# Expert attention on one core: projections regrouped on TensorE, value sums side by side, value split moved to VectorE

## What is computed

```python
ss = sigmoid(x @ Ws).reshape(b, t, H, E);  sd = sigmoid(x @ Wd).reshape(b, t, H, E)   # H=8 heads, E=5, DH=64
ms, md = topk_mask(ss, 3), topk_mask(sd, 3)
ss_g, sd_g = ss * ms, sd * md
q5 = (x @ Wq).reshape(b, t, H, E, DH)
k5, v5 = split((x @ Wkv).reshape(b, t, 2, H, E, DH))
q = einsum('bthed,bthe->bhtd', q5, sd_g)
k = einsum('bthed,bthe->bhtd', k5, ss_g)
v = einsum('bthed,bthe->bhtd', v5, ss_g)
attn = softmax(einsum('bhid,bhjd->bhij', q * DH ** -0.5, k))
out = einsum('bhij,bhjd->bihd', attn, v)
o5 = einsum('bthd,dm->bthm', out, Wo).reshape(b, t, H, E, DIM)
y = einsum('bthem,bthe->btm', o5, md)
```

## Time and profile before

| | |
|---|---|
| median of 3 runs | 2641.14 us (2640.59 to 2646.53) |
| the profiled execution, its own time | 2640.06 us |
| its span, first to last instruction | 2638.3 us |
| TensorE busy | 2353.3 us, 89% |
| VectorE busy | 2009.1 us, 76% |
| GpSimd busy | 1804.6 us, 68% |
| ScalarE busy | 1480.1 us, 56% |
| mean granted TensorE clock | 0.953 of full |

### The profile page before, as it was taken

One profiled execution on the slowest core, in us unless ns is written; L12 is line 12 of the kernel. 1 busy time (PEld: TensorE's weight loads), 2 busy tenths in 40 slices (PEclk: granted clock), 3 DMA queues, 4 the chain that ended last, 5 costly groups with the idle time before them and its releaser, 6 DMA issues. The chain is left out here.

```text
span 2638.3 us, 55375 instructions
## 1 busy us (share of the span) xinstructions
PE 2353.3 (89%) x21054; PEld 1517.7 (58%) x21054; DVE 2009.1 (76%) x3656; ACT 1480.1 (56%) x2085; POOL 1804.6 (68%) x1704
## 2 busy tenths in 40 slices
PE   6788777888799999999978999999879799999987
PEld 3555534644466667666655666666533556666655
DVE  7998555545677777777669999999567899999974
ACT  4222122332688888888834566556744256655665
POOL 0888300000699999999946899999820388999986
PEclk9899779889899999999989999999989899999999
DMA  1000000000698989889943666666710256666666
GB/s 46 1 1 0 1 24 14 1 24 17 134 160 151 163 148 162 159 151 163 145 112 64 113 113 117 119 116 113 140 40 0 70 95 117 113 119 116 117 113 122
DMA packets 829353, 243.48 MB, mean 92 GB/s; under 512 B 811528, under 2 KB 820232, under 8 KB 829088
## 3 DMA queue, kind: packets, MB, share of 16 engines
q1 hardware_dynamic: 829088, 239.93, 49.6%
HBM read 20.70 MB, written 1.05 MB: 8 GB/s over the span
## 5 line engine op out<-in xcount | busy, mean ns | idle before, releaser
L2303 PE MATMUL banks<-g_w,normed_t 128*128 128x320 f32 x1536 | 508.7, 457 | 23.9 <-DVE g_scratch L2610 11.0
L1581 POOL TENSOR_TENSOR g_p_lo<-g_p,g_p_hi 128x768 bf16<-128x768 f32 (+1 forms) x256 | 478.5, 1891 | 35.7 <-POOL g_z L2496 23.2
L1786 DVE TENSOR_REDUCE at_negmax<-banks 128x1 f32<-128x1024 f32 x256 | 301.4, 1219 | 154.6 <-PE banks L1698 154.6
L2303 PEld LDWEIGHTS banks<-g_w,normed_t 128*128 128x128 f32 x1536 | 262.3, 189 | 209.9 <-DVE g_scratch L2610 85.8
L1763 POOL TENSOR_TENSOR at_p_lo<-at_p,at_p_hi 128x640 bf16<-128x640 f32 x256 | 356.9, 1415 | 12.9 <-ACT at_p_hi L1751 11.3
L1594 DVE TENSOR_REDUCE g_negmax<-banks 128x1 f32<-128x1024 f32 x256 | 310.3, 1217 | 42.0 <-PE banks L1504 42.0
L1744 ACT ACTIVATE at_p<-banks,at_negmax 128x1024 f32<-128x1024 f32 x256 | 285.7, 1116 | 6.2 <-DVE at_negmax L1786 6.2
L1558 ACT ACTIVATE g_p<-banks,g_negmax 128x1024 f32<-128x1024 f32 x256 | 285.2, 1114 | 5.6 <-DVE g_negmax L1594 5.3
L1698 PE MATMUL banks<-at_k_t,at_q 64*128 64x512 f32 x1024 | 258.0, 622 | 18.2 <-POOL at_k_t L2047 9.5
L1504 PE MATMUL banks<-g_k_t,g_q 64*128 64x512 f32 x1024 | 254.4, 615 | 12.6 <-ACT g_p L1558 7.2
L1571 ACT CAST g_r_hi<-banks 128x256 bf16<-128x256 f32 x128 | 47.7, 372 | 380.8 <-PE banks L1515 380.8
(11 more groups left out here) (419 smaller groups left out, 5995.8 us busy)
## 6 DMA issues: line engine op xcount, KB each, us to landing
at_swapped<-at_crossed SPq DMA_DIRECT2D x128, 128.0 KB, 2.8
g_w<-in_ex_w SPq DMA_DIRECT2D x2, 2880.0 KB, 11.5
f_w<-in_W SPq DMA_DIRECT2D x2, 1024.0 KB, 5.5
at_rope<-in_rope SPq DMA_DIRECT2D x1, 2048.0 KB, 9.4
at_t_hi<-at_p_hi SPq DMA_TRANSPOSE x128, 3.7
at_t_lo<-at_p_lo SPq DMA_TRANSPOSE x128, 3.6
g_t_hi<-g_p_hi SPq DMA_TRANSPOSE x128, 4.3
g_t_lo<-g_p_lo SPq DMA_TRANSPOSE x128, 4.2
```

What stands on the lines that cost most here:

```text
L1581: self.nc.gpsimd.tensor_tensor(self.part(self.p_lo, j, h), self.p[:, j % 2, h, 0:self.WIDTH[h]], self.part(self.p_hi, j, h), ALU.subtract) ...
L1786: self.nc.vector.tensor_reduce(self.negmax[:, j % 2, h:h + 1], self.core.banks[:, first:first + 2, :], AX.XY, ALU.max, negate=True).then_i ...
L2303: nc.tensor.matmul(out[:, 0:ED], core.xt[:, at:at + P], w[:, kind * H + tile // (T * BATCH) * 2 + h, :], start=True, stop=True).then_inc(p ...
```

## The change

It sets another order in the loop's four streams.

- TensorE: the first pair goes ahead of the scores, the second behind them, both in the spare banks. The third goes into banks 0 and 1, once the first exponential of tile j + 1 has emptied them (`exp_done`). The first pair therefore waits only for the product before the last. The scores, which overwrite banks 0 and 1, wait for the third product of the step before. Both value sums follow each other ahead of the third pair. The turning goes into the spare banks, between the value sums, and waits for the second product. `subtract` comes last.
- ScalarE: the first exponential comes before `act_copy`; the placing and the second exponential move up; the cast of the values comes behind the second exponential.
- GpSimd: the values' low part is gone.
- VectorE: it takes that subtraction (`dve_split_values`, between second maximum and routing); first product and sum of values go ahead of the first maximum, the second product between the maxima.

The last unit keeps its order of `subtract`, value sums and copies.

```diff
--- before.py
+++ after.py
@@ -1617,11 +1617,6 @@
         if unit >= 2:
             act.wait_ge(self.av_done, 2 * self.T * (unit - 1))
         self.nc.scalar.copy(self.v_hi[:, unit % 2, self.half(i)], self.v[:, self.half(i)]).then_inc(self.v_split_hi, 1)
-
-    def pool_split_values(self, pool, unit, i):
-        pool.wait_ge(self.v_split_hi, 2 * unit + i + 1)
-        self.nc.gpsimd.tensor_tensor(self.v_lo[:, unit % 2, self.half(i)], self.v[:, self.half(i)], self.v_hi[:, unit % 2, self.half(i)],
-                                     ALU.subtract).then_inc(self.v_split, 1)
 
     def dve_split_values(self, dve, unit, i):
         dve.wait_ge(self.v_split_hi, 2 * unit + i + 1)
@@ -2349,23 +2344,27 @@
             for j in range(STEPS):
                 unit, t = j // T, j % T
                 turning = t in (2, 6) and unit + 1 < UNITS
-
-                def beside(k):
-                    n = first(j) + 2 * k
-                    if n < first(j + 1):
-                        pe.wait_ge(product_ready, n // 2)
-                        for h in range(2):
-                            project(n + h, spare[h])
-
+                pairs = (first(j + 1) - first(j)) // 2
                 finishing = done_in(t) if unit + 1 == UNITS else ()
+
+                def both_heads(k, banks):
+                    for h in range(2):
+                        project(first(j) + 2 * k + h, banks[h])
 
                 if j == STEPS - T:
                     pe.wait_ge(product_ready, first(STEPS) // 2)
+                if t in (3, 7) and unit + 1 < UNITS:
+                    pe.wait_ge(qk_ready, (unit + 1) * 4 + t // 4 * 2 + 2)
+                if pairs:
+                    pe.wait_ge(product_ready, first(j) // 2 - (1 if j and first(j) - first(j - 1) == 6 else 0))
+                    both_heads(0, spare)
                 if j + 1 < STEPS:
-                    if t in (3, 7) and unit + 1 < UNITS:
-                        pe.wait_ge(qk_ready, (unit + 1) * 4 + t // 4 * 2 + 2)
+                    if pairs:
+                        pe.wait_ge(product_ready, first(j) // 2)
                     hs.scores(pe, j + 1)
-                beside(0)
+                if pairs == 3:
+                    pe.wait_ge(product_ready, first(j) // 2 + 1)
+                    both_heads(1, spare)
                 hs.transpose(pe, j)
                 for k, tile in finishing[0:1]:
                     turn_out(k, tile)
@@ -2373,15 +2372,19 @@
                     project_out(*done_in(t - 1)[1])
                 if j:
                     hs.values(pe, j - 1, 0)
-                beside(1)
-                hs.subtract(pe, j)
                 if turning:
-                    pe.wait_ge(hs.exp_done, 2 * j + 3)
+                    pe.wait_ge(product_ready, first(j) // 2 + min(pairs, 2))
                     for i in range(2):
-                        turn(unit + 1, t // 4 * 2 + i, core.ps[i])
+                        turn(unit + 1, t // 4 * 2 + i, spare[i])
+                if unit + 1 == UNITS:
+                    hs.subtract(pe, j)
                 if j:
                     hs.values(pe, j - 1, 1)
-                beside(2)
+                if pairs == 3:
+                    pe.wait_ge(hs.exp_done, 2 * j + 3)
+                    both_heads(2, core.ps[0:2])
+                if unit + 1 < UNITS:
+                    hs.subtract(pe, j)
                 for k, tile in finishing[0:1]:
                     project_out(k, tile)
                 for k, tile in finishing[1:2]:
@@ -2450,23 +2453,26 @@
                 unit, t = j // T, j % T
                 last = j + 1 == STEPS
                 finishing = done_in(t) if unit + 1 == UNITS else ()
-                hs.act_copy(act, j)
+                if unit + 1 == UNITS:
+                    hs.act_copy(act, j)
                 for k, tile in finishing[0:1]:
                     place_out(k)
                 if not last:
                     hs.act_exp(act, j + 1, 0)
+                if unit + 1 < UNITS:
+                    hs.act_copy(act, j)
+                if t in (2, 6) and unit + 1 < UNITS:
+                    for i in range(2):
+                        place(unit + 1, t // 4 * 2 + i, core.ps[6 + i])
                 if not last:
                     hs.act_hi(act, j + 1, 0)
+                if not last:
+                    hs.act_exp(act, j + 1, 1)
                 if t == 0 and unit:
                     hs.act_split_values(act, unit, 1, (v_ready, (unit + 1) * T))
                 if t == 4 and unit + 1 < UNITS:
                     hs.act_split_values(act, unit + 1, 0, (v_ready, (unit + 1) * T + T // 2))
-                if not last:
-                    hs.act_exp(act, j + 1, 1)
                 hs.act_rest(act, j)
-                if t in (2, 6) and unit + 1 < UNITS:
-                    for i in range(2):
-                        place(unit + 1, t // 4 * 2 + i, core.ps[i])
                 if not last:
                     hs.act_hi(act, j + 1, 1)
                 for k, tile in finishing[1:2]:
@@ -2537,10 +2543,6 @@
             for j in range(STEPS):
                 for h in range(2):
                     hs.pool_lo(pool, j, h)
-                if j % T == 0 and j:
-                    hs.pool_split_values(pool, j // T, 1)
-                if j % T == 4 and j // T + 1 < UNITS:
-                    hs.pool_split_values(pool, j // T + 1, 0)
                 if j < 18 and j % 9 < 8:
                     count_duels(2 + j // 9, j % 9)
                 elif j < 18:
@@ -2680,20 +2682,24 @@
                 def beside(k):
                     n = first(j) + 2 * k
                     if n < first(j + 1):
-                        apply_gates(n, 6)
+                        apply_gates(n, 0 if k == 2 else 6)
 
                 finishing = done_in(t) if unit + 1 == UNITS else ()
 
+                beside(0)
+                if j + T < TOTAL:
+                    sum_values(j + T)
                 if j + 1 < STEPS:
                     hs.dve_max(dve, j + 1, 0)
-                beside(0)
+                beside(1)
                 if j + 1 < STEPS:
                     hs.dve_max(dve, j + 1, 1)
                 if unit + 1 == UNITS and t > 2:
                     add_out(*done_in(t - 1)[1])
-                beside(1)
-                if j + T < TOTAL:
-                    sum_values(j + T)
+                if t == 0 and unit:
+                    hs.dve_split_values(dve, unit, 1)
+                if t == 4 and unit + 1 < UNITS:
+                    hs.dve_split_values(dve, unit + 1, 0)
                 if j:
                     route(j - 1)
                 beside(2)
```

## The result

| | before | after |
|---|---|---|
| median | 2643.3 us (4 runs beside after's) | 2700.56 us (2695.86 to 2700.78, 4 runs) |
| ratio, 95% interval | | 1.0212 [1.0194, 1.023] |
| the profiled execution, its span | 2640.06, 2638.3 us | 2695.86, 2694.1 us |
| TensorE, VectorE busy | 2353.3, 2009.1 us | 2353.3, 2024.6 us |
| GpSimd, ScalarE busy | 1804.6, 1480.1 us | 1772.6, 1468.6 us |

A forecast was written before the change was run, and what follows sets the result against it. A closed round over TensorE and VectorE was taken to bound the step, VectorE alone afterwards. Shorter ordinary steps, less turning and splitting costs, made both loops +18 (2658 us); clock falls added 25: 2683 us, range 2646 to 2710.

The forecast's parts named there:

- The ordinary step: Loop step without turning or splitting: VectorE alone sets it, 7.3 us instead of 7.71.
- The turning step: Steps t = 2 and 6: eight transposes between the value sums delay VectorE's reciprocal by 0.9 to 1.0, 8.25 us.
- The splitting step: Steps t = 4 and, from unit 1, t = 0: VectorE's subtraction waits for ScalarE's late cast, 2.5 us more.
- the idle before the subtraction: Sign on VectorE: about 1.8 us idle, released by ScalarE's copy of the values, 26 to 28 times.
- Taking 0.70 and not 1.22: Subtraction's length on VectorE: 0.69 taken, GpSimd then waiting for the routing; 1.22 beside GpSimd would add 14 us.
- The clock: TensorE's 2.7 us holes lower its clock: 18 of 26 counted, 1.4 us each, +25 us.
- The second loop: Second expert attention loop, about 1.5 us longer before the change: +8.3 against the first loop's +9.8.
- In the last 11 steps ... nothing net: Loop's end: the split at j = 56 costs up to 2.5 us, but GpSimd's longest chain is relieved: nothing net.
- the wait that I had said would not come back: Value sums' wait for transposed low parts of the probabilities: these land 2.0 into a step, due at 3.4.
- On GpSimd the removed split gives nothing back: In splitting steps, taking the values' split off GpSimd saves no time.
- my second rival: Stall, clock fall, and VectorE meets GpSimd: subtraction 1.22 (+14) or ordinary step 7.4 (+11); 2694 to 2710, chance 0.16.

The follow-up runs named there:

- The filler: Changed kernel plus two unused fp32 matmuls of 512 columns where TensorE would stand empty, filling 24 of 26 holes: 2677.34 us, ratio 1.0119.

## Why the prediction was right, and where it was short

Forecast 2683 (2646 to 2710), measured 2700.56: slower, as said, 18 us above. Term by term, each against its own step in the prediction:

- **The ordinary step**, forecast 7.3, is 7.21, and 7.28 behind a splitting one. The second and third pairs wait for nothing beyond VectorE's round, and no value sum waited for its operands in the 53 steps. Right.
- **The turning step**, forecast 8.25, is 8.43. The reciprocal waits 0.78 us for the second value sum, as forecast, but this isn't what sets the step. The third product is done at 1674.37, and the scores come at 1674.63, without idle time right behind the first pair: TensorE's own order, with the eight transposes behind a wait of 0.25 us for the second product, is the longer way. The forecast took VectorE's. The run with the turning moved agrees: the reciprocal's wait is gone, and the step is still 8.40.

```profile
1672.39 0.17 DVE L1601 RECIPROCAL g_recip<-banks 128x2 f32<-128x2 f32 x1 [0.78 <-PE banks L1545]
...
1673.55 0.82 DVE L2612 TENSOR_TENSOR g_scratch<-banks,g_gate 128x640 f32<-128x640 f32 x1
...
1673.45 1.24 PE L2298 MATMUL banks<-g_w,normed_t 128*128 128x320 f32 x4
1674.63 1.56 PE L1504 MATMUL banks<-g_k_t,g_q 64*128 64x512 f32 x6
```

- **The splitting step**, forecast 9.8, is 9.86; the idle before the subtraction, forecast about 1.8, is 1.84. One of the 13, at j = 8, has 11.29; the same step was long before the change too (8.98): VectorE's mask comparison stands there, 1.51 us long in both kernels. The run that moves only the cast confirms the cause. Taking 0.70 and not 1.22 was right, for the reason given: GpSimd was waiting for the routing (2.28 us in that step).
- **The clock**, forecast 18 falls of 1.4, +25: 24 of the 26 holes were followed by one. Of the steps behind them 20 grew by 1.36 to 1.60, 1.42 in the mean, the two at j = 17 by only 0.15 and 0.21, since they take 8.70 even at the upper clock: the second mask comparison stands there, 1.50 us long instead of 0.35 before, and two fell into the last nine steps. The filler shows 27.9 in the 53 steps of both loops, 2.9 over the forecast. The size was right. The count was too small, and came near by luck: four of the 24 falls cost next to nothing in these steps or lie behind them.
- **The second loop** was forecast to lose 1.5 less, since it had been that much longer; it lost 24.7 us in the 53 steps and the first one 26.1. Right.
- **"In the last 11 steps ... nothing net"** is the step that failed: +4.1 and +2.9. The late cast stalls VectorE at j = 56 too, and with it the routing and GpSimd, whose chain sets these steps. The waits of 1895 to 1926 show where it surfaces, as the wait that I had said would not come back:

```profile
PE banks L1545 <- DMA g_t_lo<-g_p_lo: 4.2, 2, 3.0
```

  With the cast first the nine steps take 62.4 and 62.4, so the late cast is the cause (ahead of the second exponential it still costs there: 66.0 and 64.4). A part is the clock: the step j = 53, behind the last of the 13 holes, takes 7.97 us, and 6.82 with either earlier cast, where the clock holds. The filler says nothing here, since it leaves that hole open (65.2 and 65.1 us for the nine steps). Behind the 3.0 us wait above the clock fell too; what that cost wasn't taken apart.
- **The lead-in** was not in the sum: +1.35 in each loop, in every kernel with the new order. The first pair now stands ahead of the scores of tile 1; that this is the reason was not tried apart.
- **"On GpSimd the removed split gives nothing back"** was too strong: in the old order it was worth 4.8 and 7.1 us a loop (turning steps 113.2 and 115.3 us, 108.4 and 108.2 with the split moved); 3.4 of the 7.1 are a single step of 12.14, behind whose wait the clock fell.

In sum the loops lost 60.5 where 43 was forecast, 17.5 more: 4.9 in the 53 steps without the clock, 2.9 more clock, 7.0 in the last steps, 2.7 in the lead-ins. The program outside them was 4.7 shorter in the profiled execution. The measured time lies among the numbers of my second rival, but neither of its mechanisms was at work.

## What to carry to other kernels

An instruction moved to the engine that bounds the loop should find its input ready: here 0.7 us of work cost 2.5 because its producer had been put behind an exponential that depends on the same engine, and moving that producer up turned a loss of 57 us into a gain of 27. When an operation is moved, follow its input's place in the producer's order as closely as its own. Price a stall in the last, thinner steps of a loop apart from the steady ones: another engine has the longest chain there, and the cover is gone.

## What the runs showed of the hardware

- A hole's length alone doesn't decide over the clock. Of 26 holes of 2.58 us in the steady steps two were followed by a clock of 1.00. In the kernel with cast first and split on GpSimd one of 2.69 us left it at 1.00 as well (windows: the hole, and what follows):

```profile
1742.30:1745.00 2.70, 0.04 (x1) 0.04 (x2) 1.96 (x3) 1.38 (x2) 2.46 (x3) 1.00 1.14 107
1745.00:1748.40 3.40, 3.40 (x60) 3.07 (x61) 0.83 (x3) 2.03 (x4) 3.09 (x4) 1.00 0.51 109
```

  The holes of 1.57 us in the steady steps were followed by no fall, nor those of 0.86. But in the last nine steps, which have little matmul work, the kernel with the cast first has a hole of 1.55 us in each loop with a fall behind it; the changed kernel has the same hole without one:

```profile
1845.00:1846.50 1.50, 0.00 (x1) 0.00 (x0) 0.51 (x2) 1.50 (x3) 0.86 (x1) 1.00 0.50 99
1846.50:1849.90 3.40, 3.34 (x10) 1.32 (x11) 0.33 (x1) 1.65 (x3) 3.14 (x3) 0.62 1.06 137
```

- The Trainium skill (TensorE: Matmul & The Clock Gate, "HAM oscillation — how this bites in real kernels") describes a kernel whose clock falls again at each DMA wait of its loop, waits of about 3 to 5 us. Here holes of 2.58 us did the same in 24 of 26 cases, at 1.42 us in a step behind them, so a shorter wait can be enough, though not every time.
- Two fp32 matmuls of 512 columns in the hole, with 0.86 us left empty, kept the clock at 2.4 GHz behind all 24 holes that they filled, at no cost to the step.
- The subtraction with both inputs in SBUF took 0.70 us with GpSimd idle, and 1.03 to 1.06 in the steady steps beside it; the longest, in the lead-in, 1.23.
- The mask comparison on VectorE (a tensor_scalar, 128x320 fp32, one tensor input in SBUF) took 0.32 us in the lead-in with GpSimd idle. It took 1.51 where it ran beside GpSimd's low parts: at j = 8 in every kernel (0.67 in one loop of one of them), and at j = 17 in the changed kernel (VectorE, then GpSimd, kernel after):

```profile
1555.49 1.50 DVE L2595 TENSOR_SCALAR g_mask<-g_mask 128x320 f32<-128x320 f32 x1
...
1555.16 3.80 POOL L1581 TENSOR_TENSOR g_p_lo<-g_p,g_p_hi 128x768 bf16<-128x768 f32 x2 [0.24 <-POOL g_z L2499]
```
